# A Perceiver layer on one core: the first slot tile of the expert stage is bound to expert 0, and that expert's weights are loaded inside routing

## The chip, the core and the metric

The kernel runs on one core of one Trainium2 chip. The metric is the time of one execution on the device, in microseconds (us). A core has five engines with an instruction stream of their own each: TensorE (PE, matrix multiplies), VectorE (DVE), ScalarE (ACT), GpSimd (POOL) and SyncE (SP, which here only issues transfers). They meet through semaphores. Transfers between HBM (the chip's memory) and SBUF (the core's memory) are moved by 16 DMA engines; matmuls write to PSUM banks.

## What is computed

`x` is 32 x 32 tokens of 512 values, `TOK` = 1024 tokens. Three sublayers follow each other, each on a layer norm of `x` and added to it:

```python
x = x + _L0_xattn_ref(_layernorm(x), ctx_768, mask, ...)     # cross-attention
x = x + _L0_attn_ref(_layernorm(x), ...)                     # gated delta rule, a scan over 32 steps
x = x + _L0_ffn_ref(_layernorm(x), router_w, gate_proj, up_proj, down_proj)
```

Only the last one is touched. It is a mixture of 8 experts, of which each token takes its best 2:

```python
probs = softmax(x @ router_w)                       # 8 experts
routing_weights, routing_idx = top_k(probs, 2)      # normalised to sum 1
gate, up = x @ gate_proj[e], x @ up_proj[e]         # 512 -> 1408, e of the token
expert_out = (silu(gate) * up) @ down_proj[e]       # 1408 -> 512
out = sum over the two of weight * expert_out
```

All in float32; one expert's three matrices are 2.9 MB each.

## The kernel before, in words

The program is a row of blocks, one after another. In a block every engine runs its own function, and at its end all engines meet at a barrier. The blocks at issue are the last three: `layer_norm` (third norm), `route` and `experts`.

**`route`.** SP loads the small router matrix. PE multiplies the tokens with it (L1343). DVE finds the two best experts of each token (`tops`), counts the tokens of each expert, and rounds the counts up to tiles of 128 slots: `tiles` is the number of tiles of each expert, `start` the first tile of each, `slot` the slot number of each (token, choice). There are at most `TILES` = 23 tiles. `hot` is a 0/1 matrix that picks the tokens of slot tile 0; `tile_expert` holds for each tile its expert and whether that differs from the tile before (`fresh`). Then the barrier.

**`experts`.** It goes over the 23 tiles, and in each over `NB` = 6 blocks of 256 columns of the 1408 (the last one 128), 138 steps `n` in all.
- POOL issues 16 indirect transfers (L1633) that scatter the normed tokens to their slots in HBM (`x_slots`), one for 128 tokens and one choice.
- PE makes the tokens of tile 0 itself, without the scatter: `pick_first` multiplies `xn3` with `hot` (L1498). ACT rounds the result to `xh` (`take_x`, L1578) and DVE makes the remainder `xl` (`split_x`, L1652). For the tiles after it SP loads the rows from `x_slots` (`load_x`, L1458), and PE transposes them (`turn_x`, L1515).
- The weights are split likewise: `split_gate_up(n)` is a cast to `gh` on ACT (L1596) and a subtraction to `gl` on DVE (L1661), through a ring of 4 buffers.
- `gate_up(n)` on PE is 12 matmuls (L1528 to L1530, 4 times each). ACT takes silu of it (L1609), DVE multiplies (`hid`, L1694), PE transposes that (`turn_h`, L1538), ACT copies it to `hT` (L1620), and PE multiplies it with the third matrix (`down`, L1551).
- SP loads an expert's weights in three groups each of `w_gu` (L1465, two transfers a group) and `w_d` (L1472), nine transfers, in the order gu0, gu1, d0, gu2, d1, d2. They are skipped where `fresh` is 0.

The order on each engine is written out by hand. On PE, step `n` is this, so that `turn_x` of tile 1 stands at step 2, in front of `gate_up(3)`:

```python
gate_up(n)
if n >= 2:
    down(n - 2)
if 1 <= n <= STEPS:
    turn_h(n - 1)
if n % NB == 2 and n // NB + 1 < TILES:
    turn_x(n // NB + 1)
```

`load_x(1)` waits on SP until all 16 scatters have landed, since a tile's rows can come from any of them. SP reads `tile_expert` at the start of each tile, so that in the kernel before no weight is loaded ahead of the barrier behind `route`. The functions follow.

Of the kernel before, what the change touches and what calls it, by code (L numbers as in the profile page):

```python
# [11 lines left out]
F32 = mybir.dt.float32  # L12
# [3 lines left out]
ALU = mybir.AluOpType  # L16
# [3 lines left out]
P = 128  # L20
B, N, C = 32, 32, 512
TOK = B * N
NT = TOK // P
BT = P // N
KC = C // P
# [16 lines left out]
E, F = 8, 1408  # L42
FC = F // P
BLK = 256
RING = 4
NB = -(-F // BLK)
TILES = (2 * TOK + E * (P - 1)) // P
# [18 lines left out]
class Chain:  # L66
# [18 lines left out]
    def link(self, ins):  # L85
        self.n += 1
        ins.then_inc(self.sem, 1)
        self.eng.wait_ge(self.sem, self.base + self.n)
# [1198 lines left out]
           "x_slots": (TILES * P, C), "y_slots": (TILES * P, C)}  # L1287


def route(nc, d, ps, xnT, weight, slot, slot_f, slot_w, tile_expert, column, hot):  # L1290


    with ExitStack() as ctx:
        sb = lambda name, shape: ctx.enter_context(nc.sbuf_tensor(name, shape, F32))
        sem = lambda name: ctx.enter_context(nc.semaphore(name))
# [4 lines left out]
        s, best, at_best, first = sb("s", [P, NT, E]), sb("best", [P, NT]), sb("at_best", [P, NT, E]), sb("first", [P, NT])  # L1300
# [13 lines left out]
        with nc.Block() as block:  # L1314
            @block.sync
            def _(sp):
                sp.dma_start(router[:, :, :], d["router_w"].rearrange("(k p) e -> p k e", p=P)).then_inc(w_in, 16)

            @block.gpsimd
            def _(pool):  # L1320
# [36 lines left out]
            def _(dve):  # L1357
# [8 lines left out]
                for rank in range(2):  # L1366
# [8 lines left out]
                    if rank == 0:  # L1375
# [15 lines left out]
                link(tt(over[:, :, :], ps[2][:, 0:E][:, :, None].to_broadcast([P, E, NT]),  # L1391
                        steps[:, None, :].to_broadcast([P, E, NT]), ALU.is_gt))
                link(red(tiles[:, :], over[:, :, :], AX.X, ALU.add))
                link(tt(cube[:, :, :], tiles[:, None, :].to_broadcast([P, E, E]), lower8[:, :, :], ALU.mult))
                link(red(start[:, :], cube[:, :, :], AX.X, ALU.add))
                link(nc.vector.scalar_tensor_tensor(pos[:, :, :], start[:, None, :].to_broadcast([P, NT, E]), float(P),
# [18 lines left out]
                    link(red(slot_w[:, r, :], picked[:, :, :], AX.X, ALU.add))  # L1415


def experts(nc, d, ps, ident, x_nat, xn3, slot, slot_f, slot_w, tile_expert, column, hot, out):

# [1 line left out]
    with ExitStack() as ctx:  # L1423
        sb = lambda name, shape, dt=F32: ctx.enter_context(nc.sbuf_tensor(name, shape, dt))
        sem = lambda name: ctx.enter_context(nc.semaphore(name))
        w_gu, w_d = sb("w_gu", [P, KC, 2, F]), sb("w_d", [P, FC, C])
        xs = [sb(f"xs{i}", [P, C]) for i in range(3)]
        xh, xl = ([sb(f"{name}{i}", [P, KC, P], F32R) for i in range(2)] for name in ("xh", "xl"))
        gh, gl = ([sb(f"{name}{i}", [P, KC, 2, BLK], F32R) for i in range(RING)] for name in ("gh", "gl"))
# [6 lines left out]
        rel = sb("rel", [P, 2, NT])  # L1436
        scattered, place_done, p_turned, p_copied, added, f_done, f_added, own = (
            sem("scattered"), sem("place_done"), sem("p_turned"), sem("p_copied"), sem("t_added"), sem("f_done"), sem("f_added"), sem("e_own"))
        x_in, gu_in, d_in = [sem(f"xs_in{i}") for i in range(3)], [sem(f"gu_in{g}") for g in range(3)], [sem(f"d_in{g}") for g in range(3)]
        x_turned, xh_done, xl_done, gu_done, silu_done, hid_done = sem("x_turned"), sem("xh_done"), sem("xl_done"), sem("gu_done"), sem("silu_done"), sem("hid_done")  # L1440
        h_turned, hT_done, d_done, y_ready = sem("h_turned"), sem("hT_done"), sem("d_done"), sem("y_ready")
        gh_done, gl_done = sem("gh_done"), sem("gl_done")
# [2 lines left out]
        GU_BANK, H_BANK, X_BANK, Y_BANK = 0, 3, 5, 6  # L1445
        STEPS = TILES * NB
        width = lambda b: min(BLK, F - b * BLK)
        group = lambda g: slice(g * 2 * BLK, min((g + 1) * 2 * BLK, F))

        with nc.Block() as block:  # L1450
            @block.sync
            def _(sp):
                def load_x(s):
                    if s == 1:
                        sp.wait_ge(scattered, 16 * 2 * NT)
                    if s >= 4:
                        sp.wait_ge(x_turned, s - 2)
                    sp.dma_start(xs[s % 3][:, :], d["x_slots"][s * P:(s + 1) * P, :]).then_inc(x_in[s % 3], 16)  # L1458

                def load_gate_up(s, e, g):  # L1460
                    if s:
                        sp.wait_ge(gl_done, (s - 1) * NB + 2 * g + 2)
                    cols = group(g)
                    for n, src in enumerate(("gate_proj", "up_proj")):
                        sp.dma_start(w_gu[:, :, n, cols],  # L1465
                                     d[src][bass.ds(e, 1), :, cols].rearrange("a (k p) f -> p (a k) f", p=P), cond=fresh).then_inc(gu_in[g], 16)

                def load_down(s, e, g):
                    if s:
                        sp.wait_ge(d_done, (s - 1) * NB + 2 * g + 2)  # L1470
                    rows = group(g)
                    sp.dma_start(w_d[:, rows.start // P:rows.stop // P, :],  # L1472
                                 d["down_proj"][bass.ds(e, 1), rows, :].rearrange("a (c p) n -> p (a c) n", p=P), cond=fresh).then_inc(d_in[g], 16)

                for s in range(TILES):
                    e = sp.value_load(tile_expert[0:1, 0, s:s + 1], min_val=0, max_val=E - 1)
                    fresh = sp.value_load(tile_expert[0:1, 1, s:s + 1], min_val=0, max_val=1)
                    if 0 < s < TILES - 1:
                        load_x(s + 1)
                    load_gate_up(s, e, 0)  # L1480
                    load_gate_up(s, e, 1)
                    load_down(s, e, 0)
                    load_gate_up(s, e, 2)
                    load_down(s, e, 1)
                    load_down(s, e, 2)
                    if s == 0:
                        load_x(1)
                for t in range(NT):
                    sp.wait_ge(f_added, t + 1)
                    sp.dma_start(out.rearrange("b n c -> (b n) c")[t * P:(t + 1) * P, :], x_nat[:, t, :]).then_inc(stored, 16)  # L1490
                sp.wait_ge(stored, 16 * NT)
# [83 lines left out]
            def _(act):  # L1575
# [20 lines left out]
                    nc.scalar.copy(gh[n % RING][:, :, :, 0:bw].rearrange("p k a f -> p (k a) f"),  # L1596
                                   w_gu[:, :, :, b * BLK:b * BLK + bw].rearrange("p k a f -> p (k a) f")).then_inc(gh_done, 1)

                split_gate_up(0)
                take_x(0)  # L1600
                split_gate_up(1)
                split_gate_up(2)
                for n in range(STEPS + 2):
                    if n < STEPS:
                        bw = width(n % NB)
# [43 lines left out]
            def _(dve):  # L1649
# [32 lines left out]
                                                       ALU.mult, ALU.add).then_inc(summed, 1)  # L1682
                        dve.wait_ge(summed, 2 * t + r + 1)

                split_gate_up(0)
                split_x(0)
                split_gate_up(1)
                for n in range(STEPS + 1):
                    if n < STEPS:
                        bw = width(n % NB)  # L1690
                        dve.wait_ge(silu_done, n + 1)
                        if n >= 2:
                            dve.wait_ge(h_turned, n - 1)
                        nc.vector.tensor_tensor(hid[n % 2][:, 0:bw], silu[n % 2][:, 0:bw], ps[GU_BANK + n % 3][:, bw:2 * bw],  # L1694
                                                ALU.mult).then_inc(hid_done, 1)
                    if n + 2 < STEPS:
                        split_gate_up(n + 2)
                    if n % NB == 2 and n // NB + 1 < TILES:
                        split_x(n // NB + 1)
                    if n == 4 * NB:  # L1700
                        places()
                    if STEPS - 3 <= n < STEPS:
                        gather_sum(n - STEPS + 3)
# [7 lines left out]
def perceiver_layer(nc, d, out):  # L1711
    with ExitStack() as ctx:
        sb = lambda name, shape, dt=F32: ctx.enter_context(nc.sbuf_tensor(name, shape, dt))
        ps = [ctx.enter_context(nc.psum_tensor(f"bank{i}", [P, 512], F32))[:, :] for i in range(8)]
        ident = sb("ident", [P, P])
        x_nat = sb("x_nat", [P, NT, C])
        mask_scale = sb("mask_scale", [P, NT])
        weight = sb("weight", [P, NT, E])
        slot = sb("slot", [P, 2 * NT], I32)
        slot_w, slot_f = sb("slot_w", [P, 2, NT]), sb("slot_f", [P, 2, NT])  # L1720
        column = sb("column", [P, P])
        tile_expert = sb("tile_expert", [P, 2, TILES], I32)
        with nc.sbuf_tensor("xnT", [P, KC, TOK], F32) as xnT, nc.sbuf_tensor("w_kg", [P, KC, H * DK], F32) as w_kg, \
                nc.sbuf_tensor("p_bias", [P, 3, HC], F32) as bias, nc.semaphore("pw_ink") as wk_in:
            def load_first_weights(sp):
                sp.dma_start(w_kg[:, :, :], d["Wk"].rearrange("(k p) n -> p k n", p=P)).then_inc(wk_in, 16)
                for n, name in enumerate(("bk", "bq", "bv")):
                    sp.dma_start(bias[:, n, :], d[name]).then_inc(wk_in, 16)

            cross_attention(nc, d, ps, ident, x_nat, xnT, mask_scale, load_first_weights)  # L1730
            delta_rule(nc, d, ps, ident, x_nat, xnT, w_kg, bias, wk_in)
        with nc.sbuf_tensor("xn3", [P, NT, C], F32) as xn3, nc.sbuf_tensor("hot", [P, NT, P], F32) as hot:
            with nc.sbuf_tensor("xnT3", [P, KC, TOK], F32) as xnT:
                layer_norm(nc, "n3_", x_nat, xnT, ident, ps, xn=xn3)
                route(nc, d, ps, xnT, weight, slot, slot_f, slot_w, tile_expert, column, hot)
            experts(nc, d, ps, ident, x_nat, xn3, slot, slot_f, slot_w, tile_expert, column, hot, out)


# [37 lines left out]
```

## Time and profile before

| what | value |
|---|---|
| median of 3 runs | 1970.72 us (1969.69 to 1972.78) |
| profiled execution, its own time | 1969.36 us |
| its span on the core | 1967.5 us |
| PE busy | 1598.5 us (81%) |
| DVE busy | 1177.0 us (60%) |
| ACT busy | 706.7 us (36%) |
| POOL busy | 94.2 us (5%) |
| `route` block, about | 1271 to 1304 us |
| `experts` block, about | 1305 us to the end |

The span is the stretch from the first to the last instruction. All times in the rows below are microseconds from its start. The share of busy time is a mean over stages with different limits; it says little of one place. The clock column tells which share of full speed (2.4 GHz) TensorE was granted.

### The profile page before, as it was taken

To read this page: it belongs to the slowest core of one execution; us is meant where nothing else is said; L and a number is where in the kernel's file an instruction comes from. 1 tells how busy PE (TensorE), PEld (TensorE's weight loads), DVE (VectorE), ACT (ScalarE), POOL (GpSimd) and SP (SyncE) were. 2 spreads that over 40 slices of the span, in tenths; PEclk is the share of its full clock that TensorE was granted. 3 is DMA by queue.
4 is the path that set the end of the run, shared out by engine and by line. 5 is a ranking of instruction groups with operands and counts; after the bars stand their busy time and mean duration, and the time that the engine had idled before them with its cause. 6 is when DMAs were issued, how large, how long until landed. Compare 5 with 4: busy or idle time off the path is not lost. (4 is left out here: it accounts for less than half of the span.)

```text
span 1967.5 us, 22035 instructions
## 1 busy us (share of the span) xinstructions
PE 1598.5 (81%) x7205; PEld 1139.8 (58%) x7205; DVE 1177.0 (60%) x2577; ACT 706.7 (36%) x1360; POOL 94.2 (5%) x262
## 2 busy tenths in 40 slices
PE   7999999999799999409600079649999999999998
PEld 3777877777677777303200056446666666666664
DVE  4355455455413777999999833335565555555555
ACT  2333333333244544300000122205555555555552
POOL 0000000000000000002111100030000000000003
PEclk9999999999899999859855569869999999999999
DMA  3211010010025135523100042045444415144104
GB/s 113 78 33 33 16 32 28 21 32 16 0 89 90 63 28 90 90 52 120 43 0 0 17 112 49 1 162 191 161 166 172 174 63 198 51 165 175 38 17 134
DMA packets 116456, 153.06 MB, mean 78 GB/s; under 512 B 47216, under 2 KB 68208, under 8 KB 116368
## 3 DMA queue, kind: packets, MB, share of 16 engines
q1 hardware_dynamic: 110640, 137.81, 23.2%
q0 software_dynamic: 2560, 8.39, 1.3%
q10 hardware_dynamic: 3168, 5.77, 0.8%
q8 instruction: 45, 0.74, 0.2%
q14 instruction: 43, 0.35, 0.1%
HBM read 250.32 MB, written 31.39 MB: 143 GB/s over the span
## 5 line engine op out<-in xcount | busy, mean ns | idle before, releaser
L1661 DVE TENSOR_TENSOR gl<-w_gu,gh 128x2048 fp32r<-128x2048 f32 x138 | 290.7, 2107 | 17.1 <-issue 16.9
L1596 ACT CAST gh<-w_gu 128x2048 fp32r<-128x2048 f32 x138 | 242.3, 1756 | 56.5 <-DMA w_gu<-in_up_proj 46.4
L1551 PE MATMUL bank<-w_d,hT 128*128 128x512 f32 x506 | 242.1, 597 | 8.2 <-ACT hT L1620 7.4
L1528 PE MATMUL bank<-gh,xh 128*128 128x512 f32 (+1 forms) x552 | 219.5, 398 | 11.8 <-issue 10.1
L1694 DVE TENSOR_TENSOR hid<-silu,bank 128x256 f32<-128x256 f32 x138 | 55.1, 399 | 257.6 <-ACT silu L1609 257.6
L1530 PE MATMUL bank<-gh,xl 128*128 128x512 f32 (+1 forms) x552 | 207.2, 375 | 0.0
L1529 PE MATMUL bank<-gl,xh 128*128 128x512 f32 (+1 forms) x552 | 207.2, 375 | 0.0
L1178 PE MATMUL bank<-o_v,o_outw 128*128 128x64 f32 x256 | 36.0, 310 | 179.8 <-DMA o_v<-scratch_v_rows 179.8
L1178 PEld LDWEIGHTS bank<-o_v,o_outw 128*128 128x128 f32 x256 | 36.1, 227 | 183.5 <-DMA o_v<-scratch_v_rows 180.6
L1551 PEld LDWEIGHTS bank<-w_d,hT 128*128 128x128 f32 x506 | 91.8, 189 | 81.1 <-issue 56.9
L1609 ACT ACTIVATE silu<-bank 128x256 f32<-128x256 f32 x138 | 50.5, 366 | 214.8 <-PE bank L1530 214.6
L550 DVE COPY probT<-bank 128x512 f32<-128x512 f32 x64 | 41.1, 682 | 139.4 <-PE bank L434 139.4
L1528 PEld LDWEIGHTS bank<-gh,xh 128*128 128x128 f32 x552 | 105.1, 190 | 33.3 <-issue 16.6
L1005 PE MATMUL bank<-w_kg,xnT 128*128 128x512 f32 x128 | 61.6, 626 | 75.0 <-DMA bg_row<-in_bg 75.0
L1530 PEld LDWEIGHTS bank<-gh,xl 128*128 128x128 f32 x552 | 104.9, 190 | 19.6
L1529 PEld LDWEIGHTS bank<-gl,xh 128*128 128x128 f32 x552 | 105.5, 191 | 14.7
L1013 ACT ACTIVATE r_root<-r_nm 128x8 f32<-128x8 f32 x32 | 6.7, 208 | 274.3 <-DVE r_nm L1091 274.3
L502 ACT ACTIVATE prob<-bank,neg_max 128x257 f32<-128x257 f32 x128 | 59.0, 474 | 86.9 <-DVE neg_max L537 86.9
L1005 PEld LDWEIGHTS bank<-w_kg,xnT 128*128 128x128 f32 x128 | 23.9, 197 | 111.0 <-DMA bg_row<-in_bg 75.2
L489 ACT COPY xv<-bank 128x512 f32<-128x512 f32 x64 | 37.6, 587 | 128.9 <-PE bank L387 128.9
L1061 DVE TENSOR_TENSOR r_prod<-r_gram,r_pr 128x512 f32<-128x512 f32 (+23 forms) x158 | 83.7, 547 | 0.0
L385 PE MATMUL bank<-xa_wkv_hi,ctx_hi 128*128 128x512 f32 x192 | 79.5, 414 | 0.6 <-PEq L280 0.6
(288 smaller groups left out, 3073.3 us busy)
## 6 DMA issues: line engine op xcount, KB each, us to landing
w_gu<-in_gate_proj SPq DMA_DIRECT2D x46, 1024.0 KB
w_gu<-in_up_proj SPq DMA_DIRECT2D x46, 1024.0 KB
w_d<-in_down_proj SPq DMA_DIRECT2D x46, 1024.0 KB
w_gu<-in_gate_proj SPq DMA_DIRECT2D x23, 768.0 KB
w_gu<-in_up_proj SPq DMA_DIRECT2D x23, 768.0 KB
w_d<-in_down_proj SPq DMA_DIRECT2D x23, 768.0 KB
ctx_raw<-in_ctxT SPq DMA_DIRECT2D x32, 385.5 KB, 3.8
scratch_gram<-gram SPq DMA_DIRECT2D x8, 768.0 KB, 3.3
```

The lines of the kernel that those rows point to most:

```text
L385: pe.matmul(bank, hi(k), other_hi(k), start=(k == 0), stop=False)
L502: nc.scalar.activation(prob[s][:, c, :], ps[c][:, 0:M], ACT.Exp, bias=neg_max[s][:, c:c + 1], accum_out=total[s][:, c:c + 1]).then_inc(exp ...
L1005: pe.matmul(ps[n % 8], xnT[:, k, t * P:(t + 1) * P], wg[:, k, hf * 512:(hf + 1) * 512], start=(k == 0), stop=False)
L1061: ins = tt(parts[x][:, a], G[:, :, lo:hi, 2, 0:cols], bc(pr[nxt % 2][:, a, :, None, 0:cols], [SG, hi - lo, cols]), ALU.mult)
L1178: mm = pe.matmul(ps[O_BANK + 2 * s + h // 8][:, (h % 8) * DK:(h % 8 + 1) * DK], outw[s][:, h, :], v_row[s][:, h, :], start=True, stop=True)
L1528: pe.matmul(bank, xh[s % 2][:, k, :], hi, start=(k == 0), stop=False)
L1529: pe.matmul(bank, xh[s % 2][:, k, :], lo, start=False, stop=False)
L1530: mm = pe.matmul(bank, xl[s % 2][:, k, :], hi, start=False, stop=(k == KC - 1))
L1551: mm = pe.matmul(bank, hT[n % 2][:, c, :], w_d[:, b * (BLK // P) + c, :], start=(b == 0 and c == 0), stop=(b == NB - 1 and c == cs[-1]))
L1596: nc.scalar.copy(gh[n % RING][:, :, :, 0:bw].rearrange("p k a f -> p (k a) f"), w_gu[:, :, :, b * BLK:b * BLK + bw].rearrange("p k a f -> ...
L1661: nc.vector.tensor_tensor(gl[n % RING][:, :, :, 0:bw].rearrange("p k a f -> p (k a) f"), w_gu[:, :, :, b * BLK:b * BLK + bw].rearrange("p ...
L1694: nc.vector.tensor_tensor(hid[n % 2][:, 0:bw], silu[n % 2][:, 0:bw], ps[GU_BANK + n % 3][:, bw:2 * bw], ALU.mult).then_inc(hid_done, 1)
```

## The change

`w_gu`, `w_d` and their semaphores are now allocated ahead of `route`, and SP issues the nine weight transfers of expert 0 in `route`, right behind the router's. For that expert to be tile 0's in every case, one DVE instruction raises `tiles[:, 0:1]` to at least 1. In `experts` SP no longer handles tile 0's weights, and `load_x(1)` is its first instruction. ACT and DVE do the first three weight splits ahead of `take_x(0)` and `split_x(0)`; the split that DVE did in step 0 is left out there.

```diff
+def load_first_expert(sp, d, w_gu, w_d, gu_in, d_in):
+    groups = weight_groups()
+    for part, g in (("gu", 0), ("gu", 1), ("d", 0), ("gu", 2), ("d", 1), ("d", 2)):
+        cut = groups[g]
+        if part == "gu":
+            for n, src in enumerate(("gate_proj", "up_proj")):
+                sp.dma_start(w_gu[:, :, n, cut], d[src][0:1, :, cut].rearrange("a (k p) f -> p (a k) f", p=P)).then_inc(gu_in[g], 16)
+        else:
+            sp.dma_start(w_d[:, cut.start // P:cut.stop // P, :],
+                         d["down_proj"][0:1, cut, :].rearrange("a (c p) n -> p (a c) n", p=P)).then_inc(d_in[g], 16)
...
                 sp.dma_start(router[:, :, :], d["router_w"].rearrange("(k p) e -> p k e", p=P)).then_inc(w_in, 16)
+                load_weights(sp)
...
                 link(red(tiles[:, :], over[:, :, :], AX.X, ALU.add))
+                link(nc.vector.tensor_scalar(tiles[:, 0:1], tiles[:, 0:1], 1.0, None, ALU.max))
...
                 def load_gate_up(s, e, g):
-                    if s:
-                        sp.wait_ge(gl_done, (s - 1) * NB + 2 * g + 2)
+                    sp.wait_ge(gl_done, (s - 1) * NB + 2 * g + 2)
...
-                for s in range(TILES):
+                load_x(1)
+                for s in range(1, TILES):
...
-                    if 0 < s < TILES - 1:
+                    if s < TILES - 1:
                         load_x(s + 1)
...
-                    if s == 0:
-                        load_x(1)
...
-                split_gate_up(0)
+                for n in range(3):
+                    split_gate_up(n)
                 take_x(0)
-                split_gate_up(1)
-                split_gate_up(2)
...
-                split_gate_up(0)
+                for n in range(3):
+                    split_gate_up(n)
                 split_x(0)
-                split_gate_up(1)
...
-                    if n + 2 < STEPS:
+                    if 0 < n < STEPS - 2:
                         split_gate_up(n + 2)
```

What each engine has in its stream shows as follows. SP's stream at the end of the block before `experts` and at its start, in the kernel before (a `TENSOR_LOAD` reads `tile_expert` into a register, an `ISA` row is register work):

```order
L1317 DMA router<-in_router_w 128x4x8
L1314 UNCONDITIONAL_BRANCH
L1451 UNCONDITIONAL_BRANCH
L1476 TENSOR_LOAD tile_expert
...
L1465 DMA w_gu<-in_gate_proj 128x4x512
L1465 DMA w_gu<-in_up_proj 128x4x512
...
L1472 DMA w_d<-in_down_proj 128x3x512
L1458 DMA xs<-scratch_x_slots 128x512
```

And in the changed kernel, the same place on SP:

```order
L1335 DMA router<-in_router_w 128x4x8
L1302 DMA w_gu<-in_gate_proj 128x4x512
L1302 DMA w_gu<-in_up_proj 128x4x512
...
L1304 DMA w_d<-in_down_proj 128x3x512
L1332 UNCONDITIONAL_BRANCH
L1470 UNCONDITIONAL_BRANCH
L1477 DMA xs<-scratch_x_slots 128x512
```

The nine weight transfers moved from behind the branch that ends `route` (L1314, now L1332) to ahead of it, and nothing stands ahead of the load of tile 1's rows any more.

DVE's stream at the start of `experts`, in the kernel before:

```order
L1648 UNCONDITIONAL_BRANCH
L1661 TENSOR_TENSOR gl<-w_gu,gh 128x2048
L1652 TENSOR_TENSOR xl<-bank,xh 128x512
L1661 TENSOR_TENSOR gl<-w_gu,gh 128x2048
L1694 TENSOR_TENSOR hid<-silu,bank 128x256
L1661 TENSOR_TENSOR gl<-w_gu,gh 128x2048
L1694 TENSOR_TENSOR hid<-silu,bank 128x256
L1661 TENSOR_TENSOR gl<-w_gu,gh 128x2048
L1694 TENSOR_TENSOR hid<-silu,bank 128x256
L1661 TENSOR_TENSOR gl<-w_gu,gh 128x2048
L1652 TENSOR_TENSOR xl<-bank,xh 128x512
```

And in the changed kernel:

```order
L1663 UNCONDITIONAL_BRANCH
L1676 TENSOR_TENSOR gl<-w_gu,gh 128x2048 x3
L1667 TENSOR_TENSOR xl<-bank,xh 128x512
L1709 TENSOR_TENSOR hid<-silu,bank 128x256 x2
L1676 TENSOR_TENSOR gl<-w_gu,gh 128x2048
L1709 TENSOR_TENSOR hid<-silu,bank 128x256
L1676 TENSOR_TENSOR gl<-w_gu,gh 128x2048
L1667 TENSOR_TENSOR xl<-bank,xh 128x512
```

Three subtractions now stand in a row ahead of the first `xl`, and five in all, as before, ahead of the second; ACT's casts moved in the same way. PE's and POOL's streams in `experts` are the same rows in the same order.

## Rows read from the trace of the kernel before

**Rows 1.** Windows of the span: busy us of each engine, clock, DMA share, GB/s.

```profile
1400.00:1500.00 100.00, 98.99 (x407) 67.55 (x406) 61.63 (x67) 55.34 (x74) 0.00 (x0) 1.00 0.30 103
```

**Rows 2.** Timeline where `experts` starts: start, us, engine, line [idle before].

```profile
1303.98 0.22 DVE L1415 TENSOR_REDUCE slot_w<-picked 128x8 f32<-128x64 f32 x1
1304.74 9.28 PE L1498 MATMUL bank<-hot,xn 128*128 128x128 f32 x64 [8.79 <-PEq L1314]
1305.46 1.16 POOL L1633 DMA_INDIRECT scratch_x_slots<-xn,slot  x1 [32.23 <-POOLq L1314]
1306.37 0.40 SPq L1465 DMA_DIRECT2D w_gu<-in_gate_proj  x1
...
1319.21 1.90 ACT L1596 CAST gh<-w_gu 128x2048 fp32r<-128x2048 f32 x1 [29.30 <-DMA w_gu<-in_up_proj]
...
1321.01 0.58 ACT L1578 CAST xh<-bank 128x512 fp32r<-128x512 f32 x1
1321.14 2.29 DVE L1661 TENSOR_TENSOR gl<-w_gu,gh 128x2048 fp32r<-128x2048 f32 x1 [16.94 <-issue]
...
1323.35 0.68 DVE L1652 TENSOR_TENSOR xl<-bank,xh 128x512 fp32r<-128x512 f32 x1
...
1324.09 0.79 PE L1528 MATMUL bank<-gh,xh 128*128 128x512 f32 x1 [10.06 <-issue]
```

**Rows 3.** Timeline of SP and PE: the router's load, the weights' last issues.

```profile
1270.97 0.40 SPq L1317 DMA_DIRECT2D router<-in_router_w  x1
...
1274.79 1.45 PE L1343 MATMUL bank<-router,xnT 128*128 128x8 f32 x6 [1.02 <-DMA router<-in_router_w]
...
1325.89 5.97 SPq L1472 DMA_DIRECT2D w_d<-in_down_proj  x2
```

**Rows 4.** Timeline of DVE in `route`: the count of tiles.

```profile
1296.32 0.22 DVE L1393 TENSOR_REDUCE tiles<-over 128x8 f32<-128x64 f32 x1
```

**Rows 5.** Timeline of PE and SP: tile 1's rows, and the steps around them.

```profile
1329.30 0.40 PE L1528 MATMUL bank<-gh,xh 128*128 128x512 f32 x1
...
1333.64 1.89 SPq L1458 DMA_DIRECT2D xs<-scratch_x_slots  x2
...
1342.99 0.66 PE L1515 MATMUL bank<-ident,xs 128*128 128x128 f32 x4 [1.00 <-DMA xs<-scratch_x_slots]
...
1343.40 0.48 PE L1528 MATMUL bank<-gh,xh 128*128 128x512 f32 x1
...
1346.24 1.88 PE L1551 MATMUL bank<-w_d,hT 128*128 128x512 f32 x4
```

**Rows 6.** Timeline of POOL and DVE: the last scatters beside a split.

```profile
1322.14 2.12 POOL L1633 DMA_INDIRECT scratch_x_slots<-xn,slot  x1 [0.30 <-issue]
...
1323.95 2.28 DVE L1661 TENSOR_TENSOR gl<-w_gu,gh 128x2048 fp32r<-128x2048 f32 x1
...
1324.57 2.50 POOL L1633 DMA_INDIRECT scratch_x_slots<-xn,slot  x1 [0.30 <-issue]
...
1327.37 0.96 POOL L1633 DMA_INDIRECT scratch_x_slots<-xn,slot  x1 [0.30 <-issue]
```

**Rows 7.** The same engines near the end, where POOL issues gathers.

```profile
1933.69 2.26 POOL L1644 DMA_INDIRECT xn<-scratch_y_slots,slot  x1 [0.30 <-issue]
...
1932.83 2.28 DVE L1661 TENSOR_TENSOR gl<-w_gu,gh 128x2048 fp32r<-128x2048 f32 x1
```

**Rows 8.** Landing times of the loads of L1458, then of the gathers of L1644.

```profile
DMA to landing us min/median/max: 2.6/2.8/9.3
...
DMA to landing us min/median/max: 3.4/4.0/4.6
```

**Rows 9.** Windows with the granted clock of TensorE (third value from the end).

```profile
1308.00:1309.00 1.00, 1.00 (x8) 1.00 (x7) 0.00 (x0) 0.00 (x0) 0.80 (x1) 0.63 0.97 279
...
1318.00:1320.00 2.00, 0.00 (x0) 0.00 (x0) 0.00 (x0) 0.79 (x1) 1.39 (x3) 0.74 1.05 418
...
1329.00:1330.00 1.00, 1.00 (x5) 0.83 (x4) 0.00 (x0) 1.00 (x1) 0.00 (x0) 0.89 1.06 416
...
1340.00:1342.00 2.00, 1.99 (x6) 0.75 (x5) 1.71 (x2) 1.19 (x2) 0.00 (x0) 1.00 0.96 354
```

More of the change, by code:

```diff
@@ L1287, with weight_groups, route @@
            "x_slots": (TILES * P, C), "y_slots": (TILES * P, C)}
-def route(nc, d, ps, xnT, weight, slot, slot_f, slot_w, tile_expert, column, hot):
+def weight_groups():
+    return [slice(g * 2 * BLK, min((g + 1) * 2 * BLK, F)) for g in range(-(-F // (2 * BLK)))]
+def load_first_expert(sp, d, w_gu, w_d, gu_in, d_in):
[8 more added lines that the diff above has]
+                         d["down_proj"][0:1, cut, :].rearrange("a (c p) n -> p (a c) n", p=P)).then_inc(d_in[g], 16)
+def route(nc, d, ps, xnT, weight, slot, slot_f, slot_w, tile_expert, column, hot, load_weights):
     with ExitStack() as ctx:
@@ L1415, in _, with experts @@
                     link(red(slot_w[:, r, :], picked[:, :, :], AX.X, ALU.add))
-def experts(nc, d, ps, ident, x_nat, xn3, slot, slot_f, slot_w, tile_expert, column, hot, out):
+def experts(nc, d, ps, ident, x_nat, xn3, slot, slot_f, slot_w, tile_expert, column, hot, w_gu, w_d, gu_in, d_in, out):
     with ExitStack() as ctx:
@@ L1425, in experts @@
         sem = lambda name: ctx.enter_context(nc.semaphore(name))
-        w_gu, w_d = sb("w_gu", [P, KC, 2, F]), sb("w_d", [P, FC, C])
         xs = [sb(f"xs{i}", [P, C]) for i in range(3)]
@@ L1438, in experts @@
             sem("scattered"), sem("place_done"), sem("p_turned"), sem("p_copied"), sem("t_added"), sem("f_done"), sem("f_added"), sem("e_own"))
-        x_in, gu_in, d_in = [sem(f"xs_in{i}") for i in range(3)], [sem(f"gu_in{g}") for g in range(3)], [sem(f"d_in{g}") for g in range(3)]
+        x_in = [sem(f"xs_in{i}") for i in range(3)]
         x_turned, xh_done, xl_done, gu_done, silu_done, hid_done = sem("x_turned"), sem("xh_done"), sem("xl_done"), sem("gu_done"), sem("silu_done"), sem("hid_done")
@@ L1447, in experts @@
         width = lambda b: min(BLK, F - b * BLK)
-        group = lambda g: slice(g * 2 * BLK, min((g + 1) * 2 * BLK, F))
+        groups = weight_groups()
         with nc.Block() as block:
@@ L1460, in load_gate_up @@
                 def load_gate_up(s, e, g):
-                    if s:
-                        sp.wait_ge(gl_done, (s - 1) * NB + 2 * g + 2)
-                    cols = group(g)
+                    sp.wait_ge(gl_done, (s - 1) * NB + 2 * g + 2)
+                    cols = groups[g]
                     for n, src in enumerate(("gate_proj", "up_proj")):
@@ L1468, in load_down @@
                 def load_down(s, e, g):
-                    if s:
-                        sp.wait_ge(d_done, (s - 1) * NB + 2 * g + 2)
-                    rows = group(g)
+                    sp.wait_ge(d_done, (s - 1) * NB + 2 * g + 2)
+                    rows = groups[g]
                     sp.dma_start(w_d[:, rows.start // P:rows.stop // P, :],
                                  d["down_proj"][bass.ds(e, 1), rows, :].rearrange("a (c p) n -> p (a c) n", p=P), cond=fresh).then_inc(d_in[g], 16)
-                for s in range(TILES):
+                load_x(1)
+                for s in range(1, TILES):
                     e = sp.value_load(tile_expert[0:1, 0, s:s + 1], min_val=0, max_val=E - 1)
                     fresh = sp.value_load(tile_expert[0:1, 1, s:s + 1], min_val=0, max_val=1)
-                    if 0 < s < TILES - 1:
+                    if s < TILES - 1:
                         load_x(s + 1)
@@ L1731, in perceiver_layer @@
             delta_rule(nc, d, ps, ident, x_nat, xnT, w_kg, bias, wk_in)
-        with nc.sbuf_tensor("xn3", [P, NT, C], F32) as xn3, nc.sbuf_tensor("hot", [P, NT, P], F32) as hot:
+        with nc.sbuf_tensor("xn3", [P, NT, C], F32) as xn3, nc.sbuf_tensor("hot", [P, NT, P], F32) as hot, \
+                nc.sbuf_tensor("w_gu", [P, KC, 2, F], F32) as w_gu, nc.sbuf_tensor("w_d", [P, FC, C], F32) as w_d:
+            gu_in, d_in = ([ctx.enter_context(nc.semaphore(f"{n}_in{g}")) for g in range(len(weight_groups()))] for n in ("gu", "d"))
             with nc.sbuf_tensor("xnT3", [P, KC, TOK], F32) as xnT:
                 layer_norm(nc, "n3_", x_nat, xnT, ident, ps, xn=xn3)
-                route(nc, d, ps, xnT, weight, slot, slot_f, slot_w, tile_expert, column, hot)
-            experts(nc, d, ps, ident, x_nat, xn3, slot, slot_f, slot_w, tile_expert, column, hot, out)
+                route(nc, d, ps, xnT, weight, slot, slot_f, slot_w, tile_expert, column, hot,
+                      lambda sp: load_first_expert(sp, d, w_gu, w_d, gu_in, d_in))
+            experts(nc, d, ps, ident, x_nat, xn3, slot, slot_f, slot_w, tile_expert, column, hot, w_gu, w_d, gu_in, d_in, out)
 def kernel(**inputs):
```

## The prediction

> **What bounds the kernel now.** I first read the windows. From the middle of the expert stage on PE is busy 98.99 of 100 us at full clock [rows 1], so whatever is gained or lost before that stretch reaches the end of the program one to one; the tail behind it starts from the last tiles' stores and shifts with them. The change touches only the start of the stage, so I read its timeline next. PE's `pick_first` starts at 1304.74 and takes 9.28 us, to 1314.02. Then PE is idle for 10.06 us, until 1324.09 [rows 2]. What ends that wait is read from the other engines: ACT's first cast waits for the weights until 1319.21 (issued from 1306.37 on), takes 1.90, `xh` follows at 1321.01, DVE's `gl` at 1321.14, and `xl` at 1323.35 takes 0.68; PE starts as that ends [rows 2]. So the first weights' transfer is what PE waits for.
>
> The second place is `turn_x(1)`. PE does it at 1342.99 after a wait of 1.00 us for the DMA of tile 1's rows [rows 5]. Those rows are loaded only when all 16 scatters of POOL have landed: the last scatter starts at 1327.37 [rows 6] and SP issues the load at 1333.64 [rows 5]. `gate_up(3)` stands behind `turn_x(1)` on PE, so the scatter is a second path into the stage, today almost exactly as late as PE's own. The question is what is left of it when the first path gets short.
>
> **The change, first path.** The nine transfers are now issued behind the router's, from about 1271.4 [rows 3]. SP's issuing took from 1306.37 [rows 2] to 1325.89 + 5.97 = 1331.86 [rows 3], that is 25.5 us with the scatters beside it. Moved to 1271.4, it ends at the latest at 1296.9, 7 us before DVE's last instruction in `route` (1303.98 + 0.22) [rows 2], so SP doesn't hold up the barrier. The first group landed 12.8 us after its issue (1306.37 to 1319.21); now it is there by about 1285, and the second, even if twice as late, by 1297. Moving them costs something in two places. The router's transfer may share the DMA engines with the first weights; PE waits 1.02 us for it [rows 3], so all of a delay shows. It is issued first, so I take 0 and keep up to 1 us. The added DVE instruction works on 128x1; its neighbour on 128x64 took 0.22 [rows 4] and the chain waits for each, so 0.25 on the path. The block starts 0.25 later.
>
> ACT can cast from 1305.0 on. Casts at 1.90 and subtractions at 2.28 follow each other on DVE from about 1306.95 to 1313.8 (three times 2.28), so both engines are free when `pick_first` ends at 1304.74 + 0.25 + 9.28 = 1314.3. Then `xh` 0.58, `xl` 0.68, and gaps of about 0.1 in all: PE starts `gate_up(0)` at 1315.7 instead of 1324.09, 8.4 us earlier. The table load that ACT needs before its first silu falls into the wait for `gate_up(0)`.
>
> From there PE does three `gate_up`, one `down` (1.88 [rows 5]) and two small transposes (about 0.4 each with their gaps) until `turn_x(1)`. A `gate_up` took from 1343.40 to 1346.24, 2.84 us, at full clock [rows 5], and from 1324.09 [rows 2] to 1329.30 [rows 5], 5.21 us, at the low one. So PE reaches `turn_x(1)` at 1315.7 + 8.5 + 1.9 + 0.8 = 1326.9, or 1334.0 if all three ran low.
>
> **The change, second path.** Here the change costs. POOL's issues of a scatter take 0.96 us and follow each other after 0.30 [rows 6], 1.27 a piece. Two of the last took 2.12 and 2.50 [rows 6]. The first began at 1322.14, inside the subtraction of 1321.14 to 1323.43 [rows 2], and ended at 1324.26; the second at 1324.57, inside that of 1323.95 to 1326.23 [rows 6], and ended at 1327.07. In the tail one of 2.26 from 1933.69 ended at 1935.95, beside a subtraction of 1932.83 to 1935.11 [rows 7]. In each of the three POOL ends 0.83 to 0.84 us behind the end of DVE's instruction: it was held until that was over. Before, two subtractions fell into the scatter and cost 1.16 + 1.54 = 2.7 us. Now the first three do, back to back, and those of steps 1 and 2 (`gl(3)`, `gl(4)`) too, since PE is early.
>
> Followed: POOL's first issue runs at 1305.71. The second asks at about 1307.1, is held until 1309.24 (2.1 us), the third until 1311.5 (1.0), the fourth until 1313.8 (1.0). `gl(3)` at about 1322.0 and `gl(4)` at about 1325.2 hold one each, by 1.0 to 2.3, say 1.8. In all 4.1 + 3.6 = 7.7 us against 2.7. The last issue starts at 1327.37 + 0.25 + 5.0 = 1332.6.
>
> From the last issue to the load of tile 1's rows passed 6.27 us (1327.37 to 1333.64), with the DMA engines saturated by weights. They will be idle now. The nearest rows for that are the gathers, 3.4 to 4.6, median 4.0 [rows 8]. I take 4.0, bounds 3.4 and 6.3. The load itself took 9.3 behind the weights, otherwise 2.6 or 2.8 [rows 8]; I take 2.8. So `turn_x(1)` starts at 1332.6 + 4.0 + 2.8 = 1339.4, against 1342.99: 3.6 us earlier, and PE is idle for some 12 us ahead of it.
>
> The Trainium skill, "SBUF — State Buffer", section "SBUF: two separate sides", says that VectorE (with two SBUF inputs) and GpSimd take one port pair as an exclusive lock, held for a whole instruction, the loser blocked. The trace agrees (0.84 us behind DVE's end, three times). It does not say who goes next when DVE's instructions follow without a gap; should DVE keep it through all three, the second issue would be held until 1313.8 (6.7 us for 4.1), an estimate from the rows, and the sum would be 2.6 us worse.
>
> **The clock.** TensorE was at 0.63 of full speed on average at 1308 to 1309, so it came up about 3.9 us after `pick_first` started; it fell within 1318 to 1320, some 5 us after that ended; and it rose again within 1329 to 1330, 5.0 us after `gate_up(0)` started [rows 9]. From 1340 on it is full [rows 9]. After an idle of 12 us it will be low at 1339.4, for 3.9 to 5.0 us more. At the low clock the work of that time takes 5.21/2.84 as long, so 45% of it is lost: 1.8 to 2.3 us, I take 2.0. Before, `gate_up(3)` ran at full clock, and the low stretches lay ahead of 1343 where they are already in its time.
>
> **The sum.** 3.6 - 2.0 = 1.6 us gained of the profiled execution's 1969.36, which is 1967.8. It lies 1.4 us below the median of the runs, so the median should become 1970.72 - 1.6 = 1969.1. Its own range: blocks on POOL 6.2 to 8.7 (in place of 7.7), landing 3.4 to 6.3, clock 1.8 to 2.3, router 0 to 1: gain between 4 and -3, hardly all at once; 1967 to 1972.
>
> A kernel can't be told from an unchanged one within 0.2%, which is 3.9 us here.
>
> **Rivals.**
> - *The scatter is held less.* The issues slip between DVE's instructions, as most did before, and end only as late as before plus 0.25 at 1327.6. For it: three cases are few. Against it: each subtraction of 2.28 is longer than POOL's 1.27 period, so it can't be passed without meeting it. Then `turn_x(1)` is at 1327.6 + 6.8 = 1334.4, 8.6 earlier, less 2.0 for the clock: 6.6 gained, 1964.1. With intermediate cases 4 to 9. Chance 0.24.
> - *The scatter hardly counts.* Should scatters land in about 3 us and be held hardly at all, PE would stall only for a few us and keep its clock; nearly all of the first path comes through, 8.4 plus about 2 for the clock of the first steps: about 10, 1960.7. Chance 0.07.
> - *The second path eats more than all.* `turn_x(1)` later than 1341.0 makes the kernel slower, since the clock costs 2.0. With DVE keeping the lock through the three subtractions (2.6 more), landing as long as before (6.3, 2.3 more) it starts at 1344.3, and 1.3 + 2.0 = 3.3 us are lost; with the router's 1 us on top the time is 1975. Half of that (1972 to 1975) is likelier than the whole. Chance 0.10, of which half is over 0.2%.
> - *Nothing moves*, because SP's issuing or the router's transfer in the crowd of weights delays `route` by as much as is gained. The 7 us of room at the barrier speak against it. Chance 0.04, at about 1971 to 1973.
> - The forecast itself: 0.55.
>
> **The numbers.** Faster by over 0.2% (below 1966.8): the first two rivals, 0.31, and a little of the forecast's own lower end, 0.03: 0.34. Slower by over 0.2% (above 1974.7): 0.06. Within it: 0.60. The range 1963.5 to 1972.5 takes in the forecast and most of the first rival, and leaves out the second, the slower half of the third and the first's best cases.
>
> **What would show it.** In the changed kernel: weights landed before 1300; PE's `gate_up` from about 1315.7; POOL's issues of 2 us or more four or five times instead of twice, the last starting near 1332.6; PE idle some 10 to 13 us ahead of `turn_x(1)` at about 1339, with the rows' DMA as releaser; and a clock of 0.50 for 4 to 5 us behind it. Wrong it would be if the scatter's last issue is at 1328, if the rows land in less than 6 us from there, or if the clock stays up through the gap.

## The result, and the profile after

| | median, us | range, us | runs |
|---|---|---|---|
| before | 1970.48 | 1969.44 to 1976.02 | 17 |
| changed | 1966.71 | 1964.86 to 1970.96 | 17 |

The ratio is 0.998, with a 95% interval of 0.9972 to 0.9987: a gain of 3.8 us by the medians, 2.6 to 5.5 us by the interval. That is just at the 0.2% that I had named as the border. The forecast was 1969.1 with a range of 1963.5 to 1972.5.

The profiled execution of the changed kernel was the longest of its 17 (1970.96 us, span 1969.3). It is late before the change begins: SP's router load is at 1274.53 against 1270.97 [rows 3], 3.6 us that lie in the untouched sublayers. So I count everything from POOL's first issue in `experts`, 1309.43 here and 1305.46 before [rows 2].

The chain that ended last, in order of time, of the changed kernel, where `experts` starts (start, us, what):

```profile
1309.43 1.16 POOL scratch_x_slots L1648
1310.89 2.86 POOL scratch_x_slots L1648
1314.06 1.89 POOL scratch_x_slots L1648
1316.26 1.89 POOL scratch_x_slots L1648
1318.46 0.96 POOL scratch_x_slots L1648
...
1327.30 2.73 POOL scratch_x_slots L1648
1330.34 2.66 POOL scratch_x_slots L1648
1333.30 0.96 POOL scratch_x_slots L1648
1334.57 0.96 POOL scratch_x_slots L1648
1335.83 2.71 DMA scratch_x_slots<-xn,slot
1338.55 2.63 DMA xs<-scratch_x_slots
1341.22 1.11 PE bank L1531 x4
```

From the barrier to `turn_x(1)` the chain is now the scatter and nothing else: 16 issues, the landing of the last, the load of tile 1's rows. Five issues took 1.89 to 2.86 us in place of 0.96.

The timeline of the changed kernel shows what was beside them, and where PE is:

```profile
1308.72 10.21 PE L1514 MATMUL bank<-hot,xn 128*128 128x128 f32 x64 [8.98 <-PEq L1332]
1308.69 5.50 ACT L1612 CAST gh<-w_gu 128x2048 fp32r<-128x2048 f32 x3 [15.01 <-PEq L1332]
1310.62 4.49 DVE L1676 TENSOR_TENSOR gl<-w_gu,gh 128x2048 fp32r<-128x2048 f32 x2 [2.45 <-ACT gh L1612]
...
1320.33 0.50 PE L1544 MATMUL bank<-gh,xh 128*128 128x512 f32 x1 [1.40 <-DVE xl L1667]
...
1326.91 2.29 DVE L1676 TENSOR_TENSOR gl<-w_gu,gh 128x2048 fp32r<-128x2048 f32 x1
...
1329.88 2.29 DVE L1676 TENSOR_TENSOR gl<-w_gu,gh 128x2048 fp32r<-128x2048 f32 x1
...
1330.64 0.38 PE L1554 MATMUL bank<-ident,hid 128*128 128x128 f32 x2
1341.22 1.11 PE L1531 MATMUL bank<-ident,xs 128*128 128x128 f32 x4 [10.20 <-DMA xs<-scratch_x_slots]
1341.99 0.77 PE L1544 MATMUL bank<-gh,xh 128*128 128x512 f32 x1
...
1346.40 1.88 PE L1567 MATMUL bank<-w_d,hT 128*128 128x512 f32 x4
```

The reader is to see three things. Casts and subtractions now run under `pick_first`, and the wait of 10.06 us ahead of `gate_up(0)` [rows 2] is down to 1.40. The two later subtractions, at 1326.91 and 1329.88, end 0.83 us ahead of the ends of the two long issues (1330.03 and 1333.00): 1326.91 + 2.29 = 1329.20 and 1329.88 + 2.29 = 1332.17. And the idle time came back at `turn_x(1)`: 10.20 us.

Windows of the changed kernel (busy us of PE, PEld, DVE, ACT, POOL, then granted clock, DMA share, GB/s):

```profile
1295.00:1300.00 5.00, 1.45 (x6) 1.36 (x6) 3.92 (x13) 0.00 (x0) 0.00 (x0) 0.50 0.92 341
1300.00:1305.00 5.00, 0.00 (x0) 0.00 (x0) 4.62 (x14) 0.00 (x0) 0.00 (x0) 0.50 0.01 2
...
1325.00:1330.00 5.00, 5.00 (x22) 3.75 (x22) 3.08 (x4) 3.93 (x6) 4.39 (x3) 1.00 0.40 157
...
1335.00:1340.00 5.00, 0.00 (x0) 0.00 (x0) 0.00 (x0) 0.00 (x0) 1.49 (x2) 0.51 0.44 155
1340.00:1345.00 5.00, 3.78 (x11) 3.19 (x12) 0.69 (x1) 0.59 (x1) 0.00 (x0) 0.50 0.31 93
1345.00:1350.00 5.00, 5.00 (x20) 3.37 (x20) 1.56 (x2) 2.45 (x3) 0.00 (x0) 0.96 0.00 0
```

The weights are through by 1300, 8 us ahead of the barrier. The clock is full while PE does steps 0 to 2. It falls inside the gap, and behind the gap it is half of full speed; by the matmuls' spacing (0.43 us, then 0.23) it comes back at about 1345.3.

### The profile page after: what moved, and what is told of

Its sections match the earlier page's. It is cut to its first block and busy times, and to the rows that moved or that the text cites. A ratio compares the mean times of both kernels' runs of the same rounds, so it can differ in the third digit from the quotient of the medians.

```text
span 1969.3 us, 22016 instructions
## 1 busy us (share of the span) xinstructions
PE 1598.4 (81%) x7205; PEld 1141.5 (58%) x7205; DVE 1178.1 (60%) x2578; ACT 706.7 (36%) x1360; POOL 98.7 (5%) x262
```

## The experiments

Six kernels, each timed beside the kernel before: 5 executions each of e2, e4 and e5, 10 of e3, 12 of e1 and e6. The traces are compared by the time from POOL's first issue.

### e1: the early loads alone

The splits go back to the order of the kernel before; only the loads stay early. The diff shows ACT's stream and the condition on DVE; ahead of step 0, DVE again does one split in front of `split_x(0)` and one behind it.

```diff
-                for n in range(3):
-                    split_gate_up(n)
+                split_gate_up(0)
                 take_x(0)
+                split_gate_up(1)
+                split_gate_up(2)
...
-                    if 0 < n < STEPS - 2:
+                    if n + 2 < STEPS:
                         split_gate_up(n + 2)
```

> The changed kernel with its early loads, but with the weight splits in the order of the kernel before (one ahead of xh and xl, the second behind, the third in step 0), so that the loads alone are tried. Theory (the scatter decides, and each subtraction holds one of GpSimd's issues to its end): still five subtractions meet the scatter, one of them from the block's start, the others with gaps between them, so each holds an issue by about 1 to 2 us; the last issue starts within 1 us of the changed kernel's 26.4 us behind the first, the transposes of tile 1 likewise, and the time is that of the changed kernel within 1 us, 1966 to 1967.5 us. Rival (doing three splits early is part of the gain): 2 us or more slower than the changed kernel.

Measured: 1966.86 us, ratio 0.9976 (0.9968 to 0.9985), 0.15 us from the changed kernel. The last issue starts 26.6 us behind the first (26.4 in the changed kernel), though the long issues are others: one of 2.86 at the start, then 2.84, 2.27, 2.22 and 2.04, together 12.2 us where the changed kernel has 12.0. PE has small new waits (it starts its third `gate_up` after 0.55 us on DVE's `gl`), all in front of the gap at `turn_x(1)`. So as long as the scatter is what PE waits for, moving the splits is worth nothing, and the moved loads are the whole gain.

The gaps between the subtractions also show which issues are held. Timeline of this kernel:

```profile
1316.89 0.96 POOL L1649 DMA_INDIRECT scratch_x_slots<-xn,slot  x1 [0.31 <-issue]
...
1317.31 2.28 DVE L1677 TENSOR_TENSOR gl<-w_gu,gh 128x2048 fp32r<-128x2048 f32 x1
```

This subtraction begins 0.42 us inside an issue, and neither takes longer than alone. The next issue starts at 1318.15, inside the subtraction, and takes 2.27 us.

### e2: two subtractions behind the scatter

DVE does `gl(3)` and `gl(4)` when all scatters have landed. PE needs the first of them only behind `turn_x(1)`.

```diff
-                    if 0 < n < STEPS - 2:
+                    if n == 2:
+                        dve.wait_ge(scattered, 16 * 2 * NT)
+                        split_gate_up(3)
+                    if 1 < n < STEPS - 2:
                         split_gate_up(n + 2)
```

> The changed kernel, but VectorE does the subtractions of steps 1 and 2 (gl(3), gl(4)) only when all scatters have landed, so that three and not five of them meet GpSimd's issues. Theory (the issues are held, and the landed scatter decides when tile 1's rows come): in the changed kernel the last issue starts 62.1 us after the block's first (two issues of 2.73 and 2.66 lie in it) - counted from the first issue, 1335.83 - 1309.43 = 26.4 us; now 26.4 - 1.77 - 1.70 = 22.9 us, the transposes of tile 1 start 3.5 us earlier, and the kernel is 3 to 3.5 us faster than the changed one, 1963.4 us. Rival (the landed scatter is not what the transposes wait for, or the long issues are GpSimd's own): the last issue stays at 26 us, time unchanged or, since the subtractions now come late, 1 to 2 us slower.

("62.1 us" in it is a slip; the count that holds is the 26.4 behind it.)

Measured: 1963.37 us, ratio 0.996 (0.9947 to 0.9973), 3.3 us below the changed kernel's median. Timeline of this kernel:

```profile
1309.07 1.16 POOL L1648 DMA_INDIRECT scratch_x_slots<-xn,slot  x1 [32.67 <-POOLq L1332]
...
1332.01 0.96 POOL L1648 DMA_INDIRECT scratch_x_slots<-xn,slot  x1 [0.30 <-issue]
1334.73 2.14 SPq L1477 DMA_DIRECT2D xs<-scratch_x_slots  x2
...
1337.57 1.12 PE L1531 MATMUL bank<-ident,xs 128*128 128x128 f32 x4 [8.20 <-DMA xs<-scratch_x_slots]
```

The last issue starts 22.9 us behind the first, as worked out from the two long issues of the changed kernel. It is followed by the same 2.72 us of landing and 2.84 to `turn_x(1)`. ACT's casts of the same steps still run beside the scatter (at 1322.06 and 1324.78), and no issue beside them is long, so it is DVE's subtraction that holds. The last issue comes 3.5 us earlier and the median is 3.3 lower, so what the holds cost here reaches the kernel's time. The medians are of five executions here, and the two kernels' intervals just touch (0.9973 and 0.9972).

### e3: PE kept busy in the gap

```diff
+                    if n == 2:
+                        for _ in range(10):
+                            pe.matmul(ps[X_BANK], ident[:, :], xn3[:, 0, :], start=True, stop=True)
                     if n % NB == 2 and n // NB + 1 < TILES:
                         turn_x(n // NB + 1)
```

> The changed kernel, and TensorE does 10 float32 matmuls of 512 columns into a free bank ahead of tile 1's transposes, about 9.4 of the 10.2 us that it sat idle there; their result is overwritten. Theory (the idle time costs the clock, and that costs 2.0 us of work behind it): the transposes start at the same time, the 12 matmuls behind them take 2.8 instead of 4.4 us, the kernel is 1.5 to 2 us faster than the changed one, 1964.9 us. Rival (the clock falls for another reason, or the matmuls are slow because their operands come late): the matmuls stay at 4.4 us, no gain.

Measured: 1965.59 us, ratio 0.9974 (0.9965 to 0.9983). The medians give 1.1 us over the changed kernel, less than expected, and the two intervals overlap; the trace is clearer. Timeline of this kernel:

```profile
1305.22 1.16 POOL L1651 DMA_INDIRECT scratch_x_slots<-xn,slot  x1 [31.92 <-POOLq L1332]
...
1326.53 8.75 PE L1581 MATMUL bank<-xn,ident 128*128 128x512 f32 x20
...
1336.75 0.66 PE L1531 MATMUL bank<-ident,xs 128*128 128x128 f32 x4 [1.47 <-DMA xs<-scratch_x_slots]
1337.16 0.48 PE L1544 MATMUL bank<-gh,xh 128*128 128x512 f32 x1
...
1339.98 1.88 PE L1567 MATMUL bank<-w_d,hT 128*128 128x512 f32 x4
```

`turn_x(1)` starts 31.5 us behind the first issue (31.8 in the changed kernel), and `gate_up(3)` takes 2.82 in place of 4.41 us, with the transposes ahead 3.23 in place of 5.18: 1.95 us. The granted clock is 1.00 in every window from 1316 to 1345 in this kernel. The gap is what lowers the clock, and that is its price in the trace. (The 20 matmuls of L1581 are the ten calls: each shows as two.)

### e4: the transposes of tile 1 two steps later

The same condition in PE's, ACT's and DVE's stream:

```diff
-                    if n % NB == 2 and n // NB + 1 < TILES:
+                    if n % NB == (4 if n < NB else 2) and n // NB + 1 < TILES:
                         turn_x(n // NB + 1)
```

> The changed kernel, with the transposes of tile 1 (and ScalarE's and VectorE's work on them) two steps later, behind step 4 instead of step 2. Theory (the first path got 8 us shorter and the second one took nearly all of it, because the transposes stand ahead of work that doesn't need them): TensorE does two more steps, 8 us of work, before it needs tile 1's rows; 6 to 8 us faster than the changed one, 1959 to 1961 us. One thing can eat into it: ScalarE's cast of step 3 waits for the semaphore of tile 1's weights, which SyncE signals only behind the load of tile 1's rows, and the copy of hT stands behind that cast; by that a gap of some us stays, near the time at which the rows land. Rival (the weights' early load is not what gains, the scatter bounds everything): less than 2 us.

Measured: 1960.43 us, ratio 0.9953 (0.994 to 0.9966), 6.3 us below the changed kernel. The foreseen wait is there. ACT's cast for tile 1 waits for the weights' semaphore, and PE for `hT` behind it; timeline of this kernel:

```profile
1335.69 1.90 ACT L1612 CAST gh<-w_gu 128x2048 fp32r<-128x2048 f32 x1 [7.13 <-DMA w_gu<-in_up_proj]
...
1337.49 0.37 ACT L1635 COPY hT<-bank 128x256 f32<-128x256 f32 x1
...
1337.91 3.78 PE L1567 MATMUL bank<-w_d,hT 128*128 128x512 f32 x4 [5.11 <-ACT hT L1635]
```

No weights are moved there (0 GB/s from 1337 to 1345), tile 1 is still expert 0's: what was awaited is SP's turn, which stands behind its wait for the scatter. The gap of 5.11 us costs clock too: the granted clock is 0.50 from 1337 to 1343, and this `down` takes 3.78 in place of 1.88 us.

### e5: as e4, and SP handles tile 1's weights first

```diff
-                load_x(1)
                 for s in range(1, TILES):
...
+                    if s == 1:
+                        load_gate_up(s, e, 0)
+                        load_gate_up(s, e, 1)
+                        load_x(1)
+                        load_x(2)
...
```

> As the one before, and SyncE handles the first two groups of tile 1's gate and up weights ahead of the load of tile 1's rows, so that ScalarE's cast of step 3 does not wait for the scatter. Theory: TensorE no longer stalls at step 3 or 4, the wait for tile 1's rows at step 4 is under 2 us, the clock stays up; 10 us faster than the changed kernel, 1957 us. Rival (the rows of tile 1 bound it anyway): as the kernel before, within 1 us.

Measured: 1957.00 us (1955.43 to 1958.44), ratio 0.9924 (0.9912 to 0.9937). It is the fastest of all, 13.5 us below the kernel before and 9.7 below the changed one. Timeline of this kernel:

```profile
1332.16 0.96 POOL L1653 DMA_INDIRECT scratch_x_slots<-xn,slot  x1 [0.30 <-issue]
...
1334.89 0.83 SPq L1477 DMA_DIRECT2D xs<-scratch_x_slots  x2
...
1337.65 0.66 PE L1536 MATMUL bank<-ident,xs 128*128 128x128 f32 x4 [2.21 <-DMA xs<-scratch_x_slots]
```

`turn_x(1)` starts 31.7 us behind the first issue, as in the changed kernel (31.8). The rows of tile 1 come no earlier; PE has merely done two more steps by then and waits 2.21 us in place of 10.20. Two points of the expectation failed: the wait is not under 2 us, and the clock did not stay up. It was 0.94 on average at 1338 to 1339, 0.50 from 1339 to 1342, and the `down` at 1340.09 took 2.98 us in place of 1.88. So a gap of 2.21 us still costs some 1.7 us of clock: 1.1 in that `down`, and about 0.6 in the matmuls ahead of it, an estimate from six of them that follow each other after 0.21 in place of 0.12 us.

### e6: part of the weights beside the last scatters

```diff
-    for part, g in (("gu", 0), ("gu", 1), ("d", 0), ("gu", 2), ("d", 1), ("d", 2)):
+    for part, g in (("gu", 0), ("gu", 1), ("d", 0), ("gu", 2)):
...
+                sp.wait_ge(gl_done, 5)
+                for g in (1, 2):
+                    sp.dma_start(w_d[:, groups[g].start // P:groups[g].stop // P, :], ...).then_inc(d_in[g], 16)
                 load_x(1)
```

> The changed kernel, but the last two transfers of the third matrix (1.8 MB) are issued not in routing but when VectorE has done the subtraction of step 2, some 3.7 us ahead of the last scatter's issue, so that the DMA engines are full while the last scatters land. Theory (the landing took 6.27 us in the kernel before because the engines were full of weights, and 2.72 in the changed one because they were idle): the landing grows from 2.72 to between 3.5 and 6 us, the load of tile 1's rows stays near 2.7 if the weights are through by then or grows by what is left of them; the transposes start 1 to 4 us later and the kernel loses that, 1968 to 1970 us. Rival (the landing was late in the kernel before because SyncE was still busy with issues): the landing stays at 2.72 us and the time at 1966.7 us.

Measured: 1971.30 us, ratio 1.0002 (0.9992 to 1.0011), 4.6 us above the changed kernel. The gain is gone. Timeline of this kernel:

```profile
1307.80 1.16 POOL L1652 DMA_INDIRECT scratch_x_slots<-xn,slot  x1 [31.90 <-POOLq L1332]
...
1329.36 0.92 SPq L1494 DMA_DIRECT2D w_d<-in_down_proj  x2
...
1334.27 0.96 POOL L1652 DMA_INDIRECT scratch_x_slots<-xn,slot  x1 [0.30 <-issue]
1340.74 2.14 SPq L1477 DMA_DIRECT2D xs<-scratch_x_slots  x2
...
1343.40 1.11 PE L1535 MATMUL bank<-ident,xs 128*128 128x128 f32 x4 [15.21 <-DMA xs<-scratch_x_slots]
```

Window of this kernel, columns as above:

```profile
1335.00:1340.00 5.00, 0.00 (x0) 0.00 (x0) 0.00 (x0) 0.00 (x0) 0.23 (x1) 0.50 0.99 394
```

The weights were issued 4.9 us ahead of the last scatter (3.7 expected), and the DMA share is 0.99 while it lands, against 0.44 in the changed kernel's window of the same times, where next to nothing but the scatters and then tile 1's rows is moved. POOL's issues span the same 26.5 us, SP is free from 1330.3 on, and yet the landing took 6.47 us (1334.27 to 1340.74) in place of 2.72. The rival, that SP's own issues had made it late before, falls. Both numbers lie above what I had named: the landing above its 3.5 to 6 us, the time above its 1968 to 1970. What the run shows is that weights in flight make the landing late; it does not tell whether they are in the way in the DMA engines or in HBM.

### The six beside each other

In us from POOL's first issue, except the medians; "tile 0 done" is the start of ACT's first copy of `y`, in the kernel before 1364.62 - 1305.46.

| kernel | last issue starts | landing | `turn_x(1)` starts | tile 0 done | median |
|---|---|---|---|---|---|
| before | 21.9 | 6.27 | 37.5 | 59.2 | 1970.48 |
| changed | 26.4 | 2.72 | 31.8 | 55.4 | 1966.71 |
| e1 | 26.6 | 2.72 | 31.9 | 55.7 | 1966.86 |
| e2 | 22.9 | 2.72 | 28.5 | 52.4 | 1963.37 |
| e3 | 26.3 | 2.72 | 31.5 | 53.1 | 1965.59 |
| e4 | 26.2 | 2.72 | 37.9 | 50.7 | 1960.43 |
| e5 | 26.2 | 2.73 | 31.7 | 45.6 | 1957.00 |
| e6 | 26.5 | 6.47 | 35.6 | 59.4 | 1971.30 |

What is gained up to "tile 0 done" (3.8, 3.4, 6.8, 6.0, 8.5, 13.5, -0.2) is nearly what the medians gain (3.8, 3.6, 7.1, 4.9, 10.1, 13.5, -0.8). So by the medians what is gained in tile 0 reaches the end, within 1.6 us. The single traces are less even. From tile 0's first copy of `y` to the last tile's pass 587.5 us in the kernel before, 588.6 in the changed one, and 587.5 to 592.8 in e1 to e6. The largest difference is in e3, where tile 6 takes 30.9 us in place of the usual 26.9. Timeline of e3 there:

```profile
1506.05 1.90 ACT L1615 CAST gh<-w_gu 128x2048 fp32r<-128x2048 f32 x1 [4.16 <-DMA w_gu<-in_up_proj]
...
1508.28 3.66 PE L1567 MATMUL bank<-w_d,hT 128*128 128x512 f32 x4 [2.13 <-ACT hT L1638]
```

A cast waits for the next expert's weights, for 4.16 us where it is 1.51 in the kernel before and 2.29 in the changed one, and PE stalls for 2.13 us (none before, 0.26 in the changed one). One execution of each kernel can't tell whether an earlier PE causes this or whether it varies from run to run.

## Why the prediction was right, point by point

**First path.** `gate_up(0)` was to start 10.0 us behind POOL's first issue (1315.7 - 1305.71); it started at 10.9. `pick_first` took 10.21 in place of 9.28, since it ran longer at the low clock: 0.50 for its first 5.3 us and 0.67 on average at 1314 to 1315, where before the clock was up some 3.9 us after its start. This is hidden by the gap. SP's issues and the weights were through well ahead of the barrier, and PE's wait for the router was 1.15 us against 1.02 [rows 3]: the rival that the weights delay `route` is out. From the router's issue to POOL's first issue pass 34.5 us in the kernel before and 34.2 to 34.9 in the seven with early loads. The added instruction took 0.15 us, and with its neighbours' spacing 0.2 of the 0.25 allowed.

**The holds on POOL.** Forecast 7.7 us, the last issue 26.9 us behind the first; measured five long issues with 7.2 us more than their 0.96 each, and 26.4. The mechanism and the number of holds were right. Three of the five took 2 us or more, and two 1.89, where the sign I had named was four or five of 2 us or more. e2 shows that they are on the path: two holds less, 3.5 us in the trace and 3.3 in the medians.

Of the eight traces' long issues, 35 in all, each started while a subtraction ran and ended 0.82 to 0.85 us behind that subtraction's end. An issue that was already running is not held: in seven cases a subtraction began 0.20 to 0.87 us inside an issue, and the issue took 0.96 and the subtraction 2.28 or 2.29. (One issue of e5 began 0.02 us behind the start of a subtraction and was not held either.) Six issues started inside `xl`, whose inputs are a PSUM bank and `xh`, and took 0.96. With the rule of the Trainium skill ("SBUF — State Buffer", section "SBUF: two separate sides") the traces agree in two points: GpSimd's issue is held to the end of DVE's instruction, and the instruction that has only one of its inputs in SBUF does not hold it. They do not agree that the loser is blocked where GpSimd was first: the subtraction is not lengthened.

My worry, that DVE might keep the ports through three instructions in a row, did not come true. POOL's second issue ended at 1313.75, 0.85 us behind the end of the first subtraction at 1312.90, and one issue got through behind each of the three. The rival "held less" is out, and so is the one that DVE keeps the lock.

**The landing.** This term was mis-sized, and it is most of the difference. I took 4.0 us from the gathers [rows 8], with 3.4 as the lower bound; it was 2.72 or 2.73 in the changed kernel and in e1 to e5. The gathers go the other way, from HBM, and the bound should have reached below them. e6 shows why it was 6.27 before: with the DMA engines full it is 6.47. One of the signs of being wrong that I had named, "if the rows land in less than 6 us from there", did come about: `turn_x(1)` starts 2.72 + 2.67 = 5.39 us behind the last issue, where 4.0 + 2.8 was forecast. What was wrong by that sign is this term. So the 5.7 us by which `turn_x(1)` moved are three terms: the last issue 4.5 us later, the landing 3.55 shorter (I had priced that at 2.3), and the load of tile 1's rows 6.7 shorter (2.67 us to `turn_x(1)` in place of 9.35 behind the weights [rows 5]). The gain on this path is all of transfers that no longer share the DMA engines with weights, and most of it is the rows' load, for which I had the right number. For the landing e6 tests this; for the rows' load it is read from the windows alone (DMA share 0.96 at 1340 to 1342 before [rows 9]).

**The clock.** Forecast a loss of 2.0 us, measured 1.95 against e3.

**The sum.** `turn_x(1)` came 5.7 us earlier, counted from the first issue (forecast 3.6 + 0.25 for the later start, 3.85); the clock took 1.95 back. That leaves 3.8, the same as between the medians, for the 1.6 that were forecast. Of the missing 2 us, 1.3 are the landing, 0.5 the last issue, and 0.1 the load (2.67 for 2.8). The measured time, 1966.71, lies on the border to "faster by over 0.2%", to which I gave 0.34, and just below the forecast's own range of 1967 to 1972. The gain is more than twice the 1.6 us forecast. The stated range, from 7 us faster to 2 us slower than the kernel before, left the sign open, so that the time fell into it says little; what holds the mechanism up is the order of the events and the terms above.

Where did the first path's gain go (`gate_up(0)` starts 10.9 us behind POOL's first issue in place of 18.6, so 7.7 us)? Into a wait in front of `turn_x(1)`. e4 and e5 get it back by the order of instructions alone.

What stays open: e3's median gained 1.1 us where its trace gained 1.95 to 2.3, and e4's gained 10.1 where tile 0 shows 8.5. The spread of single runs (4 to 7 us) covers both. Beside the changed kernel's, e3's trace gains 2.3 us in tile 0 and takes 4.2 us longer over the later tiles; whether that is why its median gained less is open. My premise that whatever is gained early reaches the end one to one rests on one window, 1400 to 1500, in the first third of the stage and not at its middle.

## What to carry to other kernels

When a wait at the start of a stage is to be removed, look for the second path into the same stage and write down its landing time beside the first one's: here PE waited only 1.00 us for it, so most of the first path's 7.7 us could not count until the instruction that needs the second path was moved two steps back. A transfer moved away is worth something at its new place and at its old one, since what landed beside it now lands sooner. And when an instruction of DVE like this subtraction, with two inputs in SBUF and longer than the time from one issue to the next, is moved under a run of GpSimd's indirect transfers, count it as one held issue each, or place it behind the scatter, as e2 does.

## What the runs showed of the hardware

- A held issue ends 0.82 to 0.85 us behind the end of DVE's subtraction (35 cases), and behind each of three back to back exactly one issue gets through (2.86 or 2.87, 1.89, and 1.89 or 1.90 us, in all six traces of the changed order). Only an issue that starts inside a subtraction is held; where the subtraction begins 0.20 to 0.87 us inside an issue, both take as long as alone (seven cases).
- The landing of the last of 16 scatters of 256 KB is 2.72 us from the issue's start where the DMA engines carry no weights, 6.27 and 6.47 where they are full of them (DMA share 1.05 and 0.99).
- In PE's long gap (from 1331.0) the clock was still full at 1333 to 1335 and 0.51 on average over 1335 to 1340. Behind the gap it was at half for some 4 us: 12 matmuls of 512 columns took 4.41 us, 2.82 in e3. In e5 a gap of 2.21 us was enough: the clock fell at about 1338.9, when PE had been at work again for 1.2 us, and was back at about 1342.3.
